# Gate and up weights of a fused attention and feed-forward kernel: fetched in four pairs during the last attention slot, and the first gate/up slice computed earlier

## The reference

```python
def _L0_attn_ref(hidden_states, Wq, Wk, Wv, Wf, g_w, Wo):
    ...
    q = (hidden_states @ Wq.T).reshape(Bb, Tt, H, DK)
    k = (hidden_states @ Wk.T).reshape(Bb, Tt, H, DK)
    v = (hidden_states @ Wv.T).reshape(Bb, Tt, H, DV)
    f = (hidden_states @ Wf.T).reshape(Bb, Tt, H, M)
    q = jax.nn.silu(q)
    k = jax.nn.silu(k)
    v = jax.nn.silu(v)
    f = jax.nn.log_sigmoid(f) / GATE_NORM
    s = 1.0 - jnp.exp(f)
    ov = _gsa(tm(q), tm(k), tm(v), tm(s), tm(f), SCALE)
    o = jax.nn.silu(...)
    return (rms(o) * g_w) @ Wo.T

def _L0_ffn_ref(x, w_gate, w_up, w_down):
    gate = jax.nn.silu(_bitlinear(x, w_gate))
    up = _bitlinear(x, w_up)
    return _bitlinear(gate * up, w_down)

xn = _layernorm(x, axis=-1)
x = x + _L0_attn_ref(xn, ...) + _L0_ffn_ref(xn, ...)
```

## Time and profile before

| | |
|---|---|
| median of 3 runs | 1528.79 us (1525.7 to 1530.01) |
| the profiled execution | 1530.81 us |
| its span, slowest core (core 6) | 1529.3 us |
| spans of the 8 cores | 1508.4 to 1529.3 us |
| TensorE (PE) busy | 1362.6 us, 89% of the span |
| VectorE / ScalarE / POOL busy | 56% / 43% / 13% |
| stretch of the change, core 6 | about 802 to 870 us |

### The profile page before, as it was taken

How to read it: one execution, slowest core, us unless ns; L and a number is a source line. 1 busy time by engine, 2 the same in 40 slices (tenths; PEclk the granted TensorE clock), 3 DMA queues, 4 the chain that set the end, 5 groups by cost and what they waited for, 6 DMA issues and landing times.

```text
span 1529.3 us, 24179 instructions; the slowest of 8 cores (1508.4 to 1529.3 us)
## 1 busy us (share of the span) xinstructions
PE 1362.6 (89%) x7996; PEld 702.2 (46%) x7996; DVE 860.9 (56%) x1475; ACT 651.8 (43%) x1082; POOL 193.9 (13%) x225
## 2 busy tenths in 40 slices
PE   3666899888889988888887799999999999999999
PEld 1223344355556555555555344444444444444444
DVE  2454656347775577777776355544554455555543
ACT  2556222357778887787884311111111111111120
POOL 1000000001221111121212011111110111011110
PEclk9889999989999999999999999999999999999999
DMA  8999899706776666767751933233222333332322
GB/s 156 198 206 186 233 251 284 217 3 190 197 225 218 200 182 190 195 202 216 226 177 43 359 94 76 63 76 76 61 59 68 76 77 76 77 63 69 70 54 56
DMA packets 193690, 219.69 MB, mean 144 GB/s; under 512 B 125856, under 2 KB 146336, under 8 KB 192416
## 3 DMA queue, kind: packets, MB, share of 16 engines
q1 hardware_dynamic: 187664, 197.18, 48.2%
q0 software_dynamic: 5904, 20.97, 6.0%
HBM read 167.78 MB, written 29.36 MB: 129 GB/s over the span
## 4 chain that ended last, share of the span: by engine, by line
PE 70%; DMA 11%; DVE 8%; issue 5%; ACT 4%; SPq 1%; POOL 0%; DVEq 0%; ACTq 0%; POOLq 0%
PE ps L265 68%; DMA stg<-wgT 3%; DMA xin<-xp 3%; PE ps L270 2%; DVE STf L299 2%; DMA wf<-wfT 1%; DMA xin<-xr 1%; DMA gu_s<-stB 1%; DMA stg<-wuT 1%; DVE part L418 1%; DVE xnb L291 1%; ACT b_ok L282 1%; DVE b_qt L299 1%; DVE b_ok L285 1%; SPq L310 1%
## 5 line engine op out<-in xcount | busy, mean ns | idle before, releaser
L265 PE MATMUL ps<-wgu,xnTb 128*128 128x512 fp8e4 x2048 | 446.2, 379 | 0.0
L265 PEld LDWEIGHTS ps<-wgu,xnTb 128*128 128x128 bf16 x2048 | 200.5, 98 | 241.2 <-issue 1.0
L282 ACT ACTIVATE sg<-ps,ccol 128x512 f32<-128x512 f32 x128 | 86.1, 684 | 424.0 <-PE ps L265 422.9
L265 PE MATMUL ps<-wd,qT 128*128 128x512 fp8e4 x960 | 209.6, 379 | 0.0
L285 DVE TENSOR_TENSOR gu<-ps,sg 128x512 f32<-128x512 f32 x128 | 88.3, 690 | 190.1 <-PE ps L265 178.6
L265 PEld LDWEIGHTS ps<-wd,qT 128*128 128x128 bf16 x960 | 93.9, 98 | 113.3
L282 ACT ACTIVATE stg<-stg,wsc 128x1024 f32<-128x1024 f32 x96 | 109.6, 1144 | 27.5 <-DMA stg<-wuT 12.8
L265 PE MATMUL ps<-wf,xnTa 128*128 128x512 bf16 x256 | 70.1, 437 | 41.7 <-DMA wf<-wfT 25.2
L418 DVE TENSOR_REDUCE part<-stg 128x1 f32<-128x1024 f32 x64 | 77.6, 1218 | 49.2 <-DMA stg<-wgT 25.1
L303 POOL CAST b_s<-STf 128x512 bf16<-128x512 f32 x64 | 45.8, 719 | 432.6 <-DVE STf L299 319.6
L461 DVE TENSOR_SCALAR stB<-stg 128x1024 fp8e4<-128x1024 f32 x96 | 66.2, 689 | 60.0 <-ACT stg L282 49.7
(11 more groups left out here) (139 smaller groups left out, 1973.2 us busy)
## 6 DMA issues: line engine op xcount, KB each, us to landing
stg<-wgT SPq DMA_DIRECT2D x64, 512.0 KB, 6.6
stg<-wuT SPq DMA_DIRECT2D x64, 512.0 KB, 6.2
stg<-wdT SPq DMA_DIRECT2D x64, 512.0 KB, 5.3
xin<-xr SPq DMA_DIRECT2D x32, 512.0 KB, 4.5
xin<-xp SPq DMA_DIRECT2D x16, 512.0 KB, 6.4
gu_s<-stB SPq DMA_DIRECT2D x64, 128.0 KB, 5.8
at_s<-b_wo SPq DMA_DIRECT2D x32, 256.0 KB, 2.1
wgu<-gu_s POOLq DMA_DIRECT2D x8, 1024.0 KB, 17.8
```

The costliest lines, as they stand in the source:

```text
L265: return pe(lambda e: e.matmul(out=out, lhsT=lhsT, rhs=rhs, start=start, stop=stop, skip_group_check=True), *toks, mark=mark)
L282: return sc(lambda e: e.activation(out=out, in_=in_, func=func, **kw), *toks)
```

## The change

Four things: `wv` and `wq` change places, so that slices 4 and 5 of `wgu` now lie on `wq` and slices 6 and 7 on `wv`. The eight loads of `wgu` are issued in four pairs in slot 14, each behind the last matmul that reads the weight below it: pair 0 behind `F_(15,1)`, pair 1 behind `K_(15,1)`, pair 2 behind `Q_(15,1)`, pair 3 behind `V_(15,1)`. The block of eight loads at the start of the tail goes. And `gu_pe(0,0)` moves from behind `qt_dv(c,1)` to a place right behind `AT_(c)`.

```diff
-        wv = at("wv", 8192, BF16, W0 + 32768)
-        wq = at("wq", 8192, BF16, W0 + 49152)
+        wq = at("wq", 8192, BF16, W0 + 32768)
+        wv = at("wv", 8192, BF16, W0 + 49152)
...
+        def load_gu(g, tok):
+
+            for sl in (2 * g, 2 * g + 1):
+                wl_t.append(dma("wl%d" % sl, gp, wgu[:, sl * 8192:(sl + 1) * 8192],
+                                d_gu[:, sl * 8192:(sl + 1) * 8192], tok,
+                                store_t[0], store_t[1]))
...
             F_(f, 1)
+            if s == NO - 2:
+                load_gu(0, B[f]["wdone"])
...
             K_(f, 1)
+            if s == NO - 2:
+                load_gu(1, B[f]["wdone"])
...
             Q_(f, 1)
+            if s == NO - 2:
+                load_gu(2, B[f]["wdone"])
...
             V_(f, 1)
+            if s == NO - 2:
+                load_gu(3, B[f]["proj"])
...
-        for sl in range(8):
-            wl_t.append(dma("wl%d" % sl, gp, wgu[:, sl * 8192:(sl + 1) * 8192],
-                            d_gu[:, sl * 8192:(sl + 1) * 8192], B[c]["proj"],
-                            store_t[0], store_t[1]))
         AT_(c)
+        gu_pe(0, 0)
         gram(w)
...
         wd_t.append(dma("wd", gp, wd, d_wd, store_t[2], B[c]["qt1"], upd_end))
-        gu_pe(0, 0)
         qT_(c, 0)
```

More of the change, by code:

```diff
@@ L744, in F_ @@
             bk = RP.take()
-            p = proj(c, bk, wf, wf_t, h)
+            d["wdone"] = p = proj(c, bk, wf, wf_t, h)
             u = U.get(("e", h))
@@ L815, in Q_ @@
                            X[("o", c)]["xnT"], wq_t, bk.freed, mark=(kc == 7 and j == 3))
+            d["wdone"] = p
             t = act(b_QT[:, hsl(h)], bk.ap, AF.Silu, p, U.get(("QT", h)))
@@ L822, in K_ @@
             bk = RP.take()
-            p = proj(c, bk, wk, wk_t, h)
+            d["wdone"] = p = proj(c, bk, wk, wk_t, h)
             t = act(heads(b_KV[:, h * 1024:(h + 1) * 1024], 2, 0), v3(bk.ap, 2), AF.Silu, p,
```

## The result

The change makes the kernel slower: 1530.73 us against 1526.55 us for the kernel before (medians of 20 runs each), 4.2 us apart. The ratio, 1.0032 with a 95% interval of 1.0017 to 1.0046, is taken over the fast runs alone, those in which no die of the chip was held at a lower clock; it makes the loss 4.9 us (2.6 to 7.0). The forecast was +4.2 us, set on a median of 3 runs that was 2.2 us higher (1528.79). The profiled execution took 1532.82 us; its slowest core is now core 0, with a span of 1531.3 us.

What follows compares the result with a forecast made beforehand. TensorE was taken to bound most of the kernel (70% of the chain of waits). Pair 0 +0.2, xin landing +4.0 and clock 0 sum to +4.2 us on 1528.79, giving 1533.0 us; range 1523 to 1539 (the forecast's own 1530.5 to 1536.5).

Steps and rivals of the forecast that it cites:

- Times of the slices: wgu pairs on POOL: issued at about 805.1, 829.5, 834.0 and 837.9; the last slices land by about 851.5.
- Cost at pair 0: Slot 14, xin of block 0 delayed by pair 0, lengthening TensorE's first stop: +0.2 us, between 0 and +1.0.
- The moved slice: gu_pe(0,0) behind AT_(c): fills a 0.50 us wait, wins 0.68 us lost at the second stop; xin issued 2.78 us later.
- Landing of xin: Block 1's load, ending TensorE's second stop: packets alternate with wd's, landing at about 864.3 instead of 860.27, +4.0 us.
- The early end: xin of block 1 lands 4.7 us after issue, TensorE restarts 6.5 us earlier; rival of xin overtaking wd, 12%.
- Clock: Slowed TensorE stretch at 1.2 GHz behind the second stop need not lengthen: 0, between -1.0 and +2 us.

Runs made afterwards that it cites:

- e1: The change, but gu_pe(0,0) back behind qt_dv(c,1), the four early pairs kept; ratio to the kernel before 1.0032.
- e2: The change, but the load of wd also waits until xin of block 1 has landed; ratio to the kernel before 0.9968.
- e8: The kernel before, but the load of wd also waits until xin of block 1 has landed; ratio to the kernel before 0.9994.
- e3: The change, but wd loaded as four 1 MB DMAs with 8 KB packets; ratio to the kernel before 0.9995.
- e11: The kernel before, with load_x(1) issued in slot 14, prep_x(1) behind gu_el(0,2), prep_x(0) behind slot 14's last state update; ratio 0.9884.
- e9: The change, with load_x(1) issued in slot 14, prep_x(1) behind gu_el(0,2), prep_x(0) behind slot 14's last state update; ratio to the kernel before 0.9990.

## Why the prediction was right

Time and direction came out: +4.2 us forecast, +4.9 (2.6 to 7.0) measured, and by the mechanism named: `wd` takes the place of `wgu` beside `xin`. The close match of the size is in part luck, as the landing below shows. By its steps:

- *Times of the slices.* The issue of pairs 1 to 3 was put at 8.4, 3.9 and 0 us before the end of V; they went out 8.4, 3.9 and 0 us ahead of pair 3 (825.33, 829.84, 833.74). Right.
- *Cost at pair 0.* Forecast +0.2. The first stop on core 0 is 5.98 us; over the cores it is 5.96 to 6.44, against 5.98 to 6.18 before. Right in size for the slowest core, up to 0.4 on others.
- *The moved slice.* From the first issue of the last `wgu` pair to that of `xin` I had 848.75 - 837.89 = 10.9 us; it is 844.87 - 833.74 = 11.1. The 0.50 us wait went, and what was won is lost at the second stop (e1: same ratio).
- *Landing of xin.* The term that decides: forecast 15.6 us after its issue, measured 16.4 on core 0 and 16.4 to 17.7 over the cores. e2 and e8 show that this is `wd`, and in the changed kernel alone; e3 shows that about half of it, 5.7 of 11.5 us on the slowest cores, is the size of its packets (in the mean of the eight cores 7.8 of 12.4). The inner working was wrong in places. I let most of the two stores' packets take their turns against `wd`. Over 844:847 they went through nearly three to one beside the last 8 KB packets of `wgu`,

```profile
q0 software_dynamic: 81, 0.66, 74.5%
q1 hardware_dynamic: 237, 0.44, 37.9%
```

  and it was `xin` itself that went packet for packet with `wd`. So `xin` had nothing left to do behind `wd`, where I had put 2.5 us: it landed within 0.2 us of it. And `wd` itself took longer than I had it: through at 861.8 - 848.56 = 13.2 us after its issue by my sum, landed after 16.4. These two errors, of 2 to 3 us each, nearly cancel.
- *The early end* (all of `xin` in one turn) did not occur. By the rule of the Trainium skill, "DMA: Bandwidth & Descriptors", section "Queues, rings and completion order", an engine drains a packet of typically 9 to 17 descriptors before it switches. The counts of 93 to 90 and of the earlier trace rows, in which each packet of the profile is one row of a transfer, do not agree with it, and the measurement decides.
- *Clock.* Forecast 0. The granted clock of core 0 was down at 0.50, 1.2 GHz, during the stop and until past 872. Two windows behind the restart (busy time of PE, PEld, DVE, ACT, POOL; granted clock; DMA share; GB/s):

```profile
870.00:872.00 2.00, 2.00 (x6) 0.66 (x5) 1.24 (x2) 1.83 (x2) 0.00 (x0) 0.50 0.59 225
872.00:874.00 2.00, 2.00 (x9) 0.87 (x8) 0.14 (x1) 0.00 (x0) 0.82 (x1) 0.86 0.02 6
```

  So it ran at the lower level for about 4.7 us behind the restart; on core 6 of the kernel before it was about 2.7 us (it was still at 0.50 over 866:868). The 16 matmuls of `gu_pe(0,3)` behind the stop take 5.34 us here against 4.36 us there, 1.0 us more, within the -1.0 to +2 given. But this differs from core to core as much as from kernel to kernel: over the eight cores they take 4.4 to 5.7 us before (mean 5.15) and 4.5 to 5.9 after (mean 5.10). So in the mean the longer stop did not make the slow stretch behind it longer, as forecast. The 0.7 us between forecast and result is well within the interval.

What the prediction did not see is the larger matter: it argued over 4 us of landing time and took the two stops of 6 and 9 us as given. Both came from where `prep_x` stood on VectorE and where `load_x(1)` was issued, and e11 shows 18 us there.

## What to carry to other kernels

When a transfer comes too late, ask what will run beside it once its present neighbour is gone. Between two queues on the same DMA engines, count packets as well as bytes. Here a small load next to one with 32 KB rows waited for every one of its packets, and a transpose of a thousand small ones next to 8 KB rows took five times as long as alone. Both were cured by issuing them while the other queue was empty, or by making the large load wait for the small one. Before loads on which no engine waits are moved, look for the load on which one does.

## What the runs showed of the hardware that was not expected

- A 512 KB load with 4 KB rows landed in 3.5 to 4.9 us with nothing large beside it (kernel before, over the cores), in 11.3 to 15.8 us beside the 8 KB packets of `wgu` (14.3 on core 6), and in 16.4 to 17.7 us beside the 32 KB packets of `wd` (the changed kernel).
- Issued 2.8 us earlier into the same contention (e1), it took 1.7 us longer to land.
- The two queues do not always share one to one. Packets of q0 to packets of q1: 93 to 90 for 32 KB against 4 KB rows, 81 to 237 for 8 KB against 2 KB rows (the stores over 844:847), 141 to 120 for the same sizes in the earlier trace rows, 484 to 977 for 8 KB rows against the transpose (e9). Why is not shown.
- A transpose of 256 KB took 3.1 us alone and 16.4 us beside `wgu` (e9), and made TensorE wait 13.48 us.
